# Where the low parts of the normalised rows are subtracted: GpSimd in place of VectorE in six of the eight batches

## The reference

```
x = x + tanh(g_xattn) * cross_attention(layernorm(x), ctx)     # 16 heads, 120 keys each, eight experts' outputs averaged, then Wo
logits = layernorm(x) @ w_gate;  best = argmax;  gate = softmax at best
place  = how many earlier rows chose the same expert; rows with place >= 100 get nothing
x = x + tanh(g_ffn) * gate * (layernorm(x) @ w_expert + b_expert)   # only rows that have a place
```

## Time and profile before

| what | us |
|---|---|
| median of 3 runs | 406.76 (406.66 to 406.85) |
| the profiled execution | 407.26 |
| its span, first to last instruction | 405.5 |
| TensorE busy | 398.0 |
| VectorE busy | 336.7 |
| ScalarE busy | 225.7 |
| GpSimd busy | 167.0 |

### The profile page before, as it was taken

How to read it: one execution, slowest core, us unless ns; L and a number is a source line. 1 busy time by engine, 2 the same in 40 slices (tenths; PEclk the granted TensorE clock), 3 DMA queues, 4 the chain that set the end, 5 groups by cost and what they waited for, 6 DMA issues and landing times.

```text
span 405.5 us, 8725 instructions
## 1 busy us (share of the span) xinstructions
PE 398.0 (98%) x3102; PEld 190.1 (47%) x3102; DVE 336.7 (83%) x683; ACT 225.7 (56%) x320; POOL 167.0 (41%) x155
## 2 busy tenths in 40 slices
PE   8999999999999999999999999999999999899996
PEld 5556664444444444444444444444444444354444
DVE  7448666986898989988998999899897689779996
ACT  5434523568556763946585485748556464776110
POOL 2026999324181157309033530813261064460371
PEclk9999999999999999999999999999999999999999
DMA  7999991464059307824950692295169016241585
GB/s 271 318 386 394 345 387 60 103 125 151 2 128 208 147 13 162 222 86 91 189 202 1 150 229 103 64 181 191 47 133 242 3 34 173 80 136 27 97 174 178
DMA packets 65901, 63.19 MB, mean 156 GB/s; under 512 B 42277, under 2 KB 45617, under 8 KB 65859
## 3 DMA queue, kind: packets, MB, share of 16 engines
q1 hardware_dynamic: 60747, 56.19, 50.4%
q0 software_dynamic: 1632, 3.49, 3.1%
q10 hardware_dynamic: 3480, 2.96, 2.2%
HBM read 29.59 MB, written 12.98 MB: 105 GB/s over the span
## 4 chain that ended last, share of the span: by engine, by line
PE 85%; DVE 7%; issue 4%; ACT 2%; DMA 1%; POOL 0%; SPq 0%; DVEq 0%; ACTq 0%
PE ps L840 68%; PE ps L456 9%; PE ps L588 3%; PE ps L405 2%; DVE xb L1567 2%; DVE bn_raw L1573 1%; DVE place_hot L1724 1%; DMA raw<-in_L_xattn_Wk_dram 1%; ACT probs L1234 1%; DVE part_lo L1625 1%; ACT mixT_hi L397 0%; PE ps L1161 0%; DVE mixT_lo L398 0%; POOL known L1930 0%; PE ps L606 0%
## 5 line engine op out<-in xcount | busy, mean ns | idle before, releaser
L1234 ACT ACTIVATE probs<-ps 120x1024 f32<-120x1024 f32 x64 | 62.0, 1023 | 20.9 <-PE ps L840 20.8
L1602 DVE TENSOR_REDUCE neg_max<-ps 128x16 bf16<-128x1920 f32 x32 | 68.8, 2149 | 3.6 <-PE ps L840 3.6
L1989 POOL TENSOR_TENSOR attn_lo<-attn,attn_hi 128x512 f16<-128x512 f32 x28 | 31.8, 1158 | 91.6 <-ACT attn_hi L1234 91.6
L840 PE MATMUL ps<-xnT_hi,wqT_hi 128*128 128x512 f16 x128 | 48.6, 380 | 0.0
L840 PE MATMUL ps<-mixT_hi,attn_hi 128*128 128x512 f16 x128 | 48.5, 379 | 0.0
L840 PE MATMUL ps<-mixT_lo,attn_hi 128*128 128x512 f16 x128 | 48.5, 379 | 0.0
L840 PE MATMUL ps<-xnT_lo,wqT_hi 128*128 128x512 f16 x128 | 48.5, 379 | 0.0
L1997 POOL TENSOR_TENSOR xb<-xb,mix_bias 128x512 f32<-128x512 f32 x32 | 39.6, 1268 | 14.2 <-DVE cb_col L1544 14.2
L1234 ACT ACTIVATE q_hi<-ps,bias_cols 128x512 f16<-128x512 f32 x32 | 22.0, 689 | 31.5 <-PE ps L840 31.5
L840 PE MATMUL ps<-q_stack,k_stack 97*120 97x512 f16 x128 | 34.6, 388 | 1.4 <-ACT probs L1234 1.0
L840 PE MATMUL ps<-probs,den_sel 120*32 120x256 f32 x512 | 34.1, 384 | 0.0
(11 more groups left out here) (278 smaller groups left out, 803.7 us busy)
## 6 DMA issues: line engine op xcount, KB each, us to landing
xb<-in_x_dram SPq DMA_DIRECT2D x8, 1024.0 KB, 6.1
q_stack<-q_hi SPq DMA_DIRECT2D x48, 128.0 KB
out_dram<-xb SPq DMA_DIRECT2D x6, 1024.0 KB, 7.2
raw<-in_L_xattn_We_dram SPq DMA_DIRECT2D x5, 1024.0 KB, 12.4
q_stack<-q_lo SPq DMA_DIRECT2D x32, 128.0 KB
xb<-in_L_xattn_We_dram SPq DMA_DIRECT2D x3, 1024.0 KB, 10.8
k_stack<-k_scratch SPq DMA_DIRECT2D x8, 360.0 KB, 4.4
k_scratch<-k_hi ACTq DMA_DIRECT2D x16, 120.0 KB, 7.0
```

What stands on the lines that cost most here:

```text
L840: return e.matmul(out_, a, b, start=start, stop=stop, **kw)
L1234: return e.activation(out_, in_, func, **kw)
L1602: e.tensor_reduce(maxed[:, :, :, g], quad[:, :, 0:NT * SK].rearrange("p j (t s) -> p t j s", t=NT), AX.X, ALU.max, negate=True).then_inc(s ...
L1989: e.tensor_tensor(attn_lo[:, g, :], attn[:, g, :], attn_hi[:, g, :], ALU.subtract).then_inc(s_alo, 1)
```

## The change

The steps x_lo leave VectorE's order for the steady iterations, and GpSimd gets a step low_rows, which does the same four subtractions in a loop. It stands behind rstd2 and ahead of the attention's low parts. The waits are the same two, for the high part of the tile and for the transposing DMA of the batch before, and the semaphore raised is the same. The iteration r = -1 stays as it is on VectorE (the rows of batch 1), and GpSimd's order gets its own list for it, with the steps that it had there.

```diff
--- before.py
+++ after.py
@@ -1757,8 +1757,8 @@
                 (logit_sum, -1, 0), (stats1, 2, 0), (stats1, 2, 1), (stats1, 2, 2), (stats1, 2, 3), (moments1, 2, 0),
                 (add_table, -2, 0), (stats2, -1, 2), (stats2, -1, 3), (moments2, -1, 0),
                 (normalise1, 2, 0), (normalise1, 2, 1), (normalise1, 2, 2), (normalise1, 2, 3),
-                (logit_gap, -1, 0), (choose, -1, 0), (logit_scale, -1, 0), (x_lo, 2, 0), (x_lo, 2, 1), (gate_mix_low, 0, 0),
-                (x_lo, 2, 2), (read_places, -1, 0), (q_low, 1, 0), (x_lo, 2, 3),
+                (logit_gap, -1, 0), (choose, -1, 0), (logit_scale, -1, 0), (gate_mix_low, 0, 0),
+                (read_places, -1, 0), (q_low, 1, 0),
 
                 (reciprocal, 0, 0), (maxima, 1, 0), (rden_low, 0, 0), (q_low, 1, 1),
                 (divide, 0, 0), (divide, 0, 1), (divide, 0, 2), (divide, 0, 3), (q_low, 1, 2), (maxima, 1, 1),
@@ -1989,6 +1989,13 @@
                 e.tensor_tensor(attn_lo[:, g, :], attn[:, g, :], attn_hi[:, g, :],
                                 ALU.subtract).then_inc(s_alo, 1)
 
+            def low_rows(b, _):
+                for t in range(NT):
+                    e.wait_ge(s_xhi, 4 * (b - 1) + t + 1)
+                    e.wait_ge(s_xtl, 16 * (b - 1))
+                    e.tensor_tensor(xn_lo[:, :, t, :], xn[:, t, :].rearrange("p (k s) -> p k s", k=NK),
+                                    xn_hi[:, :, t, :], ALU.subtract).then_inc(s_xlo, 1)
+
             def add_bias(b, _):
                 e.wait_ge(s_setv, SETV)
                 e.wait_ge(s_xn, 4 * b + 4)
@@ -2004,8 +2011,9 @@
                 e.memset(row_ix[:, :], 0).then_inc(s_clr, 1)
 
             attn_lows = [(attn_low, 0, g) for g in range(NK)]
-            batch = [(rstd1, 2, 0), (rstd2, -1, 0)] + attn_lows + [(add_bias, 1, 0)]
-            run(range(-1, 2), batch)
+            run([-1], [(rstd1, 2, 0), (add_bias, 1, 0)])
+            batch = [(rstd1, 2, 0), (rstd2, -1, 0), (low_rows, 2, 0)] + attn_lows + [(add_bias, 1, 0)]
+            run(range(0, 2), batch)
             clear_rows(0, 0)
             run(range(2, B - 2), batch)
             run([B - 2], [(rstd2, -1, 0)] + attn_lows + [(add_bias, 1, 0)])
```

## The result

The median is 414.39 us (413.96 to 414.91, 5 runs) against 406.76 us for the kernel before, whose five runs beside it gave 406.39 to 407.17. The ratio is 1.0184 [1.0173, 1.0195]: slower by 7.6 us, where 15.75 was forecast. The time lies in the range, in the stretch of rival 3.

The account below looks back on a forecast made before the run. TensorE bounds the loop, busy 36.12 of 36.20 us a batch. Removal 0, added work 0, and five stalls of 3.15 us, 15.75, give 422.5 us for the median (423.0 for the profiled execution's like); range 410 to 426.

Parts of the forecast that it names:

- rival 3: VectorE let in sooner at the choice, fewer than three blocks count: 0.3 to 2.5 us a batch, 408 to 419; chance 0.16.
- What is removed: Four subtractions a batch leave VectorE, 15.5 us in all; the freed time lengthens the wait at the reciprocal, worth 0.
- What is added, by itself: GpSimd gets 24 subtractions at 1.14 us, 27 us, in its idle stretch; nobody waits for it, cost 0.
- Where the two engines meet: During the expert's choice, a 512-element GpSimd subtraction shuts out VectorE's two-operand SBUF instructions for its whole length; slack 1.15 us.
- The row of l_dif: VectorE's l_dif inside GpSimd's power takes 0.19 us, unstretched: evidence against exclusion, discounted because that power has four elements a partition.
- rival 1: No exclusion for short two-operand VectorE instructions beside GpSimd: no change, 406.8; chance 0.12.
- The sum: Low rows and choice with count sums alternate; last sum at 212.09, TensorE's places 3.15 us late in five batches: 15.75 us.
- the term of 3.15 us: TensorE's forecast stall a batch: places start near 212.2 and not at 209.06.
- The bound of two blocks: Only two low rows get in ahead of a count sum: last sum near 209.9, 0.85 us a batch, 411.0.
- Rival 2: Faster: VectorE's end-of-batch visit for the one-hot places begins earlier, at most 1.2 us, 405.5; chance 0.02.
- Rival 4: TensorE's clock falls after stalls of 3 us: an estimated 1.6 us a batch more, 430; chance 0.04.

Follow-up runs that it names:

- e4: Kernel before with the steady batches' low rows left out, VectorE only clearing two numbers per tile: 406.94 us, ratio 1.0000.
- e1: Changed kernel with GpSimd's four subtractions made to wait for the last count sum of the choice: 407.89 us, 1.0024 of the kernel before.
- e2: Changed kernel with only tiles 0 and 1 on GpSimd, the other two back on VectorE: 409.72 us, 1.0061 of the kernel before.
- e3: Changed kernel with tiles 0 to 2 on GpSimd, tile 3 back on VectorE: 414.48 us, 1.0183 of the kernel before.
- e5: Steady low rows left out; in four batches GpSimd does three unrelated subtractions that read SBUF: 411.25 us, 1.0094 of the kernel before.
- e6: Steady low rows left out; in four batches GpSimd does three clears that only write: 407.03 us, 0.9996 of the kernel before.
- e9: Changed kernel with only tile 3 on GpSimd, tiles 0 to 2 back on VectorE: 407.03 us, 1.0000 of the kernel before.
- e7: Changed kernel with ScalarE's fourth high part made ahead of the last exponentials: 423.62 us, 1.0389 of the kernel before.

## Why the direction was right and the size was not

**What is removed: right.** Worth 0, by e4, 1.0000 [0.9991, 1.001]; only part of the freed time became a longer wait at the reciprocal, the rest stands ahead of the read of the places and of q_lo.

**What is added, by itself: right.** 27.5 us in all, 1.15 each, for 27 and 1.14 forecast; the four-piece output costs about 0.01 each at most. With the engines kept apart (e1) the run is 1.0 us slower than the kernel before, so the added work by itself costs no more than about that. The attention's low parts still wait for ScalarE, 8.65 us in the batch shown.

**Where the two engines meet: right.** Each VectorE instruction with two operands in SBUF that began during a 512-element GpSimd subtraction ended 0.02 to 0.08 us behind it in the batch shown. e2 and e3 count the holds; e5 and e6 put them down to an operation that reads, and not to one that only writes. The row of l_dif, which spoke for rival 1, was rightly put down to its small partner: beside subtractions the like of it was held in every case, top_rank with its one input (0.19 at 210.16) was not. In the changed kernel l_dif, at 209.71, again lies inside GpSimd's power over four elements a partition (208.84 to 210.02) and again takes 0.19.

**The sum: this step failed.** It had the last count sum 5.16 us behind the start of choice (206.93 to 212.09); the trace has 3.41 (210.38 to 213.79). The difference of 1.75 has two parts, and they hang together.

First, it let low row 3 hold a sum: "low row 3 (its high part is there at 210.47) to 211.72, the third sum ends 211.89". In the trace the last sum is done before that high part: 213.79 against 213.80. The high part is not late by the prediction's own times: it ends 3.42 us behind the start of choice, for 3.54 (206.93 to 210.47). It is the sums that are sooner, for the reason that follows. e3 (three tiles cost as much as four) and e9 (the fourth alone costs nothing) show that it holds nothing, and e7, where it may follow at once, shows what it would hold: 4.33 us from choice to the last sum (214.50 to 218.83), 0.92 more.

Second, it added VectorE's turns to GpSimd's time, "low row 1 takes the ports to 209.12, the first count sum ends 209.29", and so on. GpSimd doesn't feel them: four subtractions take 4.49 us in e7 with four VectorE instructions held and slipping in, and 4.52 in e1 with none; the sum gave them 5.05. That is 0.56 of the other 0.83 (4.33 against 5.16); GpSimd also starts 0.12 earlier against choice than was taken (0.38 ahead of it, not 0.26), and the last sum ends 0.15 sooner behind the last subtraction (0.22, not 0.37). This is also what let the fourth row in (worked out, not run): the sum had the second count done 3.66 us behind the start of choice (210.59), past the fourth high part, so that the fourth row could start and hold the third count. In the trace the second is done 3.01 behind it (213.39), and the last two need 0.40 more.

So the exclusion was right, and what was mis-sized is the term of 3.15 us: three instructions are held and not four, for less time; 3.15 less the 1.75 is 1.40 a batch, for 1.43 measured on TensorE and 1.5 by the time (7.6 in five). The bound of two blocks, 0.85 a batch, was near too, but it was too high for two: e2 measured 2.8 us in all, 0.57 a batch.

**Rivals.** The time falls in rival 3's stretch (0.16), but not by its reason: who gets the ports when both ask went as the sum had it, VectorE at each boundary between two subtractions, and each of the three held instructions waited to the end of one. The stated range holds the time only because it was drawn down over that rival. Rival 1 is out by the held instructions of the changed kernel, e1 and e5. Rival 2 is out: e4 frees VectorE entirely of the low rows and gains nothing. Rival 4 didn't happen here (clock 1.00 in all five batches), but e7 shows that it lay only 0.9 us a batch away.

## What to carry to other kernels

Idle time on GpSimd is not free if VectorE has two-operand SBUF instructions in it: look for what VectorE does at that very time, and whether TensorE waits for it, before work is moved. Count the holds one by one: a chain of short VectorE instructions, each waiting for the last, lost here about one GpSimd instruction per link (0.9 us of 1.13), for as many as GpSimd could issue back to back. Don't add VectorE's own short turns to GpSimd's time. Then check each link against the time at which GpSimd's next input is ready: 0.65 us decided here whether a fourth instruction is held. A wait on the chain's own semaphore removed the hold, with 1.0 us left over; GpSimd work that only writes made none.

## What the runs showed of the hardware that was not expected

- A short VectorE instruction that was held got in between two GpSimd instructions that follow each other, and cost GpSimd nothing: three subtractions in 3.38 us, four in 4.49 with four instructions held, and 4.52 in e1 with none held.
- GpSimd's memset of 1024 f32 over 100 partitions (0.9 us) held no VectorE instruction; its subtraction of 512 f32 there (1.01 us) held choice and two count sums in the batch shown.
- GpSimd's power over four elements a partition (1.12 and 1.18 us) did not hold the two-operand VectorE instruction l_dif that lay inside it (0.19 both times).
- TensorE's granted clock fell to the 1.2 GHz level behind waits of 2.1 to 2.3 us in three of five batches, at a price of some 1.7 us each, and behind none of the waits of 1.2 to 1.4 us.
